# A fused relu and gate on VectorE for the first experts, their first bias folded into the output bias, and a new prologue order

## What is computed

```python
# block 1: messages with a sensitivity weight computed from adj
sens    = exp(-(1/adj - 1)**2 / (2*0.5*0.5))
weights = where(adj < 1.0, sens, 0.0)
x = x + weights @ (ln(x) @ W + B)
# block 2: 8 experts, hidden 256, top 2
logits  = z @ Wg + bg + bias                      # z = ln(x)
combine = one_hot(top2) * softmax(top2 logits)    # 1354 x 8
h = relu(einsum('td,edh->teh', z, W1) + b1)
y = einsum('teh,ehd->ted', h, W2) + b2
x = x + einsum('ted,te->td', y, combine)
# block 3: graph attention with 3 heads and two GRU cells over adj
# block 4: 8 experts, hidden 341, top 2, silu(h1) * h3
```

## Time and profile before

| what | value |
|---|---|
| median of 3 runs | 576.27 us (575.78 to 577.69) |
| the profiled execution, its own time | 573.15 us |
| its span | 571.4 us |
| PE busy | 492.5 us, 86% of the span |
| weight loads | 306.4 us, 54% |
| DVE busy | 387.3 us, 68% |
| ACT busy | 271.6 us, 48% |
| POOL busy | 118.1 us, 21% |
| mean granted TensorE clock | 0.94 of full speed |
| chain that ended last | PE 56%, DVE 24%, ACT 10%, issue 8% |

### The profile page before, as it was taken

The page is one execution under the profiler, slowest core; times in us unless marked ns, Lnnn a source line. Parts: engine busy times, 40 slices in busy tenths (PEclk is TensorE's granted clock), DMA queues, the critical chain, the costliest instruction groups (busy, mean ns, idle before and its releaser), DMA issues.

```text
span 571.4 us, 6186 instructions
## 1 busy us (share of the span) xinstructions
PE 492.5 (86%) x1889; PEld 306.4 (54%) x1889; DVE 387.3 (68%) x715; ACT 271.6 (48%) x445; POOL 118.1 (21%) x181
## 2 busy tenths in 40 slices
PE   5564879677879999999889998998978799999997
PEld 4322535344546645455444443445545687788896
DVE  2989987756586722267568868778856966666664
ACT  5988694758765421222422122111236544454553
POOL 3000000000010000000000058730103455555554
PEclk9696699889799999999999998999988999999999
DMA  8960000000000010000000013210000000000000
GB/s 284 317 170 1 1 0 0 1 1 0 1 1 1 5 45 1 0 2 0 1 0 1 28 49 103 65 30 1 0 5 2 0 2 0 20 1 2 19 1 13
DMA packets 13076, 16.76 MB, mean 29 GB/s; under 512 B 2007, under 2 KB 8410, under 8 KB 13038
## 3 DMA queue, kind: packets, MB, share of 16 engines
q1 hardware_dynamic: 13038, 16.30, 9.1%
HBM read 15.60 MB, written 0.69 MB: 29 GB/s over the span
## 4 chain that ended last, share of the span: by engine, by line
PE 56%; DVE 24%; ACT 10%; issue 8%; POOL 1%; DVEq 0%; POOLq 0%; ACTq 0%
PE bank L1220 9%; PE bank L886 7%; PE bank L888 7%; PE bank L887 7%; PE bank L1050 4%; PE bank L1168 3%; DVE pr_ring L1818 3%; PE bank L1019 2%; PE bank L1209 2%; DVE y_units L1379 2%; DVE y_units L1368 2%; PE bank L915 2%; DVE t_units L1374 2%; DVE hr_ring L1634 2%; DVE y_units L1389 1%
## 5 line engine op out<-in xcount | busy, mean ns | idle before, releaser
L1220 PE MATMUL bank<-pr_ring,hW 128*128 128x512 f32 (+3 forms) x198 | 95.5, 568 | 7.2 <-DVE pr_ring L1818 6.7
L1818 DVE SCALAR_TENSOR_TENSOR pr_ring<-adjT,regR,bank 128x512 f32<-128x512 f32 (+3 forms) x99 | 64.9, 680 | 29.5 <-PE bank L1209 27.8
L1929 DVE TENSOR_TENSOR adjT<-adjT,bank 128x512 f32<-128x512 f32 (+1 forms) x66 | 41.2, 624 | 45.5 <-PE bank L1324 24.0
L866 ACT ACTIVATE adjT<-bank 128x512 f32<-128x512 f32 (+1 forms) x66 | 36.2, 549 | 54.1 <-PE bank L888 54.1
L886 PE MATMUL bank<-z3hi,w13hi 128*128 128x512 f32 (+4 forms) x132 | 50.8, 385 | 8.2 <-DVE pr_ring L1933 3.2
L1220 PEld LDWEIGHTS bank<-pr_ring,hW 128*128 128x128 f32 (+1 forms) x198 | 35.7, 197 | 37.0 <-issue 17.8
L915 PE MATMUL bank<-y_units,msg 128*128 128x512 f32 (+3 forms) x66 | 33.3, 638 | 20.5 <-DVE y_units L1389 20.5
L888 PE MATMUL bank<-z3hi,w13lo 128*128 128x512 f32 (+4 forms) x132 | 49.4, 374 | 0.0
L887 PE MATMUL bank<-z3lo,w13hi 128*128 128x512 f32 (+4 forms) x132 | 49.0, 371 | 0.0
L1019 PE MATMUL bank<-hr_ring,W2s 128*128 128x512 f32 (+1 forms) x96 | 46.2, 569 | 0.0
L548 POOL TENSOR_TENSOR prr_ring<-adjT,adjTr 128x512 fp32r<-128x512 f32 (+4 forms) x34 | 36.0, 1060 | 48.8 <-ACT adjTr L858 46.8
(11 more groups left out here) (272 smaller groups left out, 1039.3 us busy)
## 6 DMA issues: line engine op xcount, KB each, us to landing
stage<-in_w SPq DMA_DIRECT2D x8, 341.0 KB, 3.0
adjT<-in_adjT SPq DMA_DIRECT2D x1, 2560.0 KB
...
```

The costliest lines, as they stand in the source:

```text
L866: nc.scalar.activation(s1_buf(q)[0:r, 0:w], B_H1[q % 2][0:r, 0:w], ACT.Silu).then_inc(s["s_silu"], 1)
L1220: nc.tensor.matmul(B_ACC[:, 0:w], hW[0:r, j, k * P:(k + 1) * P], ring[0:r, 0:w], start=(k == 0 and j == 0), stop=(k == K - 1 and j == T - ...
L1818: nc.vector.scalar_tensor_tensor(out=pr_ring[0:r, 4 + p % R_RING, 0:w], in0=adjT[0:r, j, cols(c)], scalar=g_col[0:r, j, k:k + 1], in1=B_F[ ...
L1929: nc.vector.tensor_tensor(sg, sg, B_GATE1[n % 2][0:r, 0:w], ALU.mult).then_inc(s["s_gated"], 1)
```

## The change

1. **Relu and gate in one DVE operation.** relu(h + b1) equals max(h, -b1) + b1, so gate times relu is gate x max(h, -b1) plus gate x b1. DVE now computes gate x max(h, -b1) straight from the hidden bank (L1673 of the changed kernel, with `nb1` = -b1 as the scalar of each partition). The relu on ACT is gone.
2. **The gate comes from on-chip memory.** ACT copies each expert's gate out of its bank once (L753, `gate_sb`, 2 buffers, 24 copies in all). PE makes the gate of expert g + 1 in the first step of expert g, and at the start of a chunk both g and g + 1 (`ahead`).
3. **The first bias goes behind the down projection.** gate x b1 times W2 is a constant row of each expert times the gate, so it is added to b2: 16 small products of W2 and b1 on PE (`hidden_bias`, L1013, between the sums of unit 2 and unit 3), a copy on ACT (L725), a transpose on PE (`hidden_bias_rows`, L1019, between the sums of unit 4 and unit 5) and an addition on DVE (L1637, between cutoff(4) and cutoff(5)), ahead of the splitting of b2.
4. **Waits.** PE overwrites a bank of `B_H` when DVE has gated tile q - 3, no longer when ACT has read it. The ring `hr_ring` has 4 buffers instead of 6.
5. **Prologue.** SP issues the first adj transfer before x, and the second before W and B. ACT waits for POOL's first 12 constants (`const_raw`) instead of all (`const_set`), does log and inverse root of unit 0 before the squares of the centred x, and square(1) of the units behind the second of those. The small copy `sel16` on DVE moves back behind newton_product(4).
6. **Tables.** PE0, ACT0, DVE0 and the MAIN tables are written anew: tasks move by a step or two.

```diff
-RING0 = 6
+RING0 = 4
+RINGG = 2
...
 PE0 = {
-    0: [("turn", 0)], 1: [("v",)], 3: [("unit", 6)], 4: [("unit", 7)], 6: [("unit", 8)], 7: [("unit", 9)], 11: [("unit", 10), ("unit", 11)],
+    0: [("turn", 0)], 3: [("unit", 6)], 5: [("unit", 7), ("v",), ("unit", 8)], 7: [("unit", 9)], 8: [("unit", 10)], 11: [("unit", 11)],
...
+        def ahead(q):
+            g, e, m = q // M0, q // M0 % E, q % M0
+            if m:
+                return []
+            return [x for x in ((g, g + 1) if e == 0 else (g + 1,)) if x // E == g // E]
...
                 for i in range(3):
                     sp.dma_start(adjT[:, 2 * i:2 * i + 2, cols(0)],
...
+                    if i == 0:
+                        sp.dma_start(xT[:, :], xT_d).then_inc(s["x_in"], 16)
+                    if i == 1:
+                        sp.dma_start(Wl0[:, :], W_d).then_inc(s["wts0_in"], 16)
+                        sp.dma_start(rowW[0:1, 0:P], B_d).then_inc(s["wts0_in"], 16)
...
-            act.wait_ge(s["const_set"], CONSTS)
+            act.wait_ge(s["const_raw"], RAW_CONSTS)
             rec_square(0)
+            rec_log(0)
+            rec_first(0)
             square_first(0)
-            rec_log(0)
             square_first(1)
-            rec_first(0)
+            rec_square(1)
             square_first(2)
-            rec_square(1)
...
             rec_first(5)
+            act.wait_ge(s["ffn0_in"], 80)
+            nc.scalar.mul(nb1[:, :], b1c[:, :], -1.0).then_inc(s["b2_step"], 1)
+            act.wait_ge(s["b2_step"], 2)
+            nc.scalar.copy(b2t[:, :], bk[1][:, 0:2 * E]).then_inc(s["b2_step"], 1)
             argument(4)
...
-                at(act, "h_ps", q + 1)
-                at(act, "y_mm", q - RING0 + 1)
-                nc.scalar.activation(hr_ring[:, q % RING0, 0:w], B_H[q % 3][:, 0:w], ACT.Relu,
-                                     bias=b1c[:, e * M0 + m:e * M0 + m + 1]).then_inc(s["h_relu"], 1)
+                for g in ahead(q):
+                    at(act, "gate_ps", g + 1)
+                    at(act, "h_gated", (g - RINGG + 1) * M0)
+                    nc.scalar.copy(gate_sb[:, g % RINGG, 0:w], B_GATE[g % 2][:, 0:w]).then_inc(s["gate_set"], 1)
...
+            def hidden_bias():
+                pe.wait_ge(s["ffn0_in"], 80)
+                pe.wait_ge(s["msg_set"], C)
+                pe.wait_ge(s["b2_step"], 1)
+                for e in range(E):
+                    for m in range(M0):
+                        mm = nc.tensor.matmul(bk[1][:, e:2 * E:E], W2s[:, e, m, :],
+                                              b1c[:, e * M0 + m:e * M0 + m + 1].to_broadcast([P, 2]), start=(m == 0), stop=(m == M0 - 1))
+                mm.then_inc(s["b2_step"], 1)
+
+            def hidden_bias_rows():
+                pe.wait_ge(s["b2_step"], 3)
+                nc.tensor.matmul(bk[4][0:2 * E, 0:P], b2t[:, :], ident[:, :], start=True, stop=True).then_inc(s["b2_step"], 1)
...
-            sums(0)
-            sums(1)
-            for g in range(2, UNITS_C):
+            for g in range(UNITS_C):
+                if g == 3:
+                    hidden_bias()
+                if g == 5:
+                    hidden_bias_rows()
                 sums(g)
...
-                at(pe, "h_relu", q - 2)
+                at(pe, "h_gated", q - 2)
...
-                if m == 0:
+                for g in ahead(q):
                     at(pe, "gt_set", c + 1)
-                    at(pe, "h_gated", (q // M0 - 1) * M0)
-                    nc.tensor.matmul(B_GATE[q // M0 % 2][:, 0:w], sel16[:, e:e + 1].to_broadcast([P, P]), GT0[:, c % 2, 0:w],
+                    at(pe, "gate_set", g - 1)
+                    nc.tensor.matmul(B_GATE[g % 2][:, 0:w], sel16[:, g % E:g % E + 1].to_broadcast([P, P]), GT0[:, c % 2, 0:w],
                                      start=True, stop=True).then_inc(s["gate_ps"], 1)
...
             newton_step(5)
+            cutoff(4)
             dve.wait_ge(s["ffn0_in"], 80)
+            dve.wait_ge(s["b2_step"], 4)
+            nc.vector.tensor_tensor(b2x[0:2 * E, :], b2x[0:2 * E, :], bk[4][0:2 * E, 0:P], ALU.add).then_inc(s["b2_step"], 1)
+            cutoff(5)
+            dve.wait_ge(s["b2_step"], 5)
             nc.vector.tensor_copy(b2hi[:, :], b2x[:, :]).then_inc(s["b2_split"], 1)
-            cutoff(4)
-            cutoff(5)
...
-                at(dve, "gate_ps", q // M0 + 1)
-                at(dve, "h_relu", q + 1)
-                hr = hr_ring[:, q % RING0, 0:w]
-                nc.vector.tensor_tensor(hr, hr, B_GATE[q // M0 % 2][:, 0:w], ALU.mult).then_inc(s["h_gated"], 1)
+                at(dve, "gate_set", q // M0 + 1)
+                at(dve, "h_ps", q + 1)
+                at(dve, "y_mm", q - RING0 + 1)
+                if q == 0:
+                    dve.wait_ge(s["b2_step"], 1)
+                nc.vector.scalar_tensor_tensor(out=hr_ring[:, q % RING0, 0:w], in0=B_H[q % 3][:, 0:w],
+                                               scalar=nb1[:, e * M0 + m:e * M0 + m + 1], in1=gate_sb[:, q // M0 % RINGG, 0:w],
+                                               op0=ALU.max, op1=ALU.mult).then_inc(s["h_gated"], 1)
```

More of the change, by code:

```diff
@@ L112 @@
[L112 to L117 removed]
+    19: [("center", 2, 0), ("sq", 17), ("arg", 14), ("ln", 17), ("exp", 14), ("inv", 17), ("neg", 1)], 20: [("arg", 15), ("exp", 15)],
@@ L118 @@
     19: [("center", 2, 0), ("mult", 15), ("step", 15), ("sign", 16)], 20: [("mult", 16), ("cut", 14), ("step", 16)],
[L119 to L121 removed]
+    21: [("sign", 17), ("scale", 2, 0), ("cut", 15), ("mult", 17)], 22: [("step", 17), ("cut", 16)], 23: [("diag", 0), ("cut", 17)],
```

82 lines of the change are left out of this document (40 added, 42 removed).

## The result

The changed kernel takes **578.75 us** (median of 18 runs, 575.78 to 582.93) against 575.62 us before (18 runs, 572.58 to 578.25). The ratio is **1.0058, 95% interval 1.0036 to 1.0080**: slower by 3.3 us by the ratio. The forecast was 570.8 us, in the wrong direction. The profiled execution took 578.04 us, with a span of 576.3 us; PE is busy 498.5 us (87%), DVE 392.6 (68%), ACT 255.6 (44%). ACT worked 16 us less than before, and the kernel is slower.

The account below looks back on a forecast made before the run. Before 198 us it saw DVE limiting block 2's first chunk, latencies the second, PE nearly the third. Terms -0.8 + 4.0 - 3.2 - 0.5 - 4.5 - 0.5 = -5.5 took 576.27 to 570.8 us; range 564.5 to 579.

Parts of the forecast that it names:

- The folded bias: Prologue: 32 records delay ACT's copy and the chain to x1(0), a loss of 4.0 us (bounds 0 and 7.2).
- Chunk 0: Block 2, first chunk, DVE the limit: most DVE waits for relus go, gain 3.2 us (bounds -0.7 and 4.9).
- Chunk 1: Block 2, second chunk: earlier gate product shortens PE's 4.51 us wait and the half clock behind it, gain 4.5 us.
- Chunk 2: Block 2, third chunk: PE is the limit, so only 0.5 us gained (0 to 2).
- Prologue start: Start of the prologue: first adj transfer issued first lets ACT begin earlier, gain 0.8 us (bounds 0 and 2.2).
- Layer norm and router: Between chunks, 97.3 to 112 us: one wait on a relu goes, gain 0.5 us (0 to 1).
- Fused operation: Gate step on DVE: 743 ns against 683, so 0.06 us more each (bounds 0 and 2.9 us in all).
- ring of 4: Buffers between gating and down projection: the needed down projection is done a step before, so no cost.
- Block 3: Last block: new task order changes nothing, covered by PE's work; zero (bounds -1.5 and +1.5 us).
- Slower: PE is tied to DVE: Block 2 rival: banks free only after DVE gates, taking back the gain; 579.5 us if all; 20%.
- The gain and the loss cancel: Rival: fold's products at half clock lose 7.2 us, second chunk of block 2 gains only 2.2; 576.3 us, 15%.
- The clock holds: Rival: fold's products keep full clock beyond 42.6 us, some 3 us less; 567.8 us, 5%.

Follow-up runs that it names:

- start_only: Kernel before with only the new prologue start (first adj transfer ahead, ACT's new order of first squares, later sel16 cast); 575.16 us, ratio 0.9989.
- act_head: Changed kernel with unit 9's square and logarithm ahead of the first gate copies and unit 11's exponential at tile 8; 575.50 us, ratio 0.9990.
- the two kernels with WARM: late_head, without and with unit factors 12 and 13 earlier on ACT, each computing hidden products of tiles 16 and 32 five times; 570.40 and 562.21 us.
- late_head: Changed kernel with act_head's two moves and the folded bias moved into PE's later waits; 571.27 us, ratio 0.9920.
- late_head_warm: late_head with the hidden products of tiles 16 and 32 computed five times instead of once; 570.40 us, ratio 0.9894.

## Why the prediction was wrong

**The folded bias** (4.0 lost): mechanism right, with every step of the chain where it was drawn; size somewhat small. It measures 5.0 us in time. The term "the sums of unit 4, 1.9 with start" took full clock for granted: in four of the five profiles with the whole fold in this place they ran at half clock for all or most of their time, and the transposition, the addition and cutoff(5) queue behind them. A is 15.1 on average over those five, and 10.2 over the eight without it there; B, 16.1 on average against 15.5, adds 0.6. The half clock itself is not the fold's alone: in five of the eight profiles without it there, the last sums before x1(0) ran at half clock too, for some 3 us, with A 10.45 to 10.63 instead of 9.51 to 9.60. With the fold standing between the units, such a stretch costs more when it falls on unit 4. The bounds (0 to 7.2) held. "Nothing downstream hides it" held too.

**Chunk 0** (3.2 gained): the step that failed. It gained nothing, C 39.14 before and 39.15 to 39.27 in the six profiles with the changed order. Against start_only it is worse: with the same relus and a clock of 1.00 from 80 to 95 us, its two last waits were one of 0.85 us, and C is 37.43. So against that profile the change *cost* some 1.7 us here, and 1.6 of the 4.9 us that I counted on the earlier trace rows hung on the clock of one execution. The sentence at fault is "The ACT copies are one expert ahead and hide behind DVE". It weighed the length of the copies (they measure 0.58 us), not their place. An operation that waits for the router stands first in ACT's queue, where one stood that waited for nothing late, and the table puts unit 11 behind another. act_head, which moves these two places only, gives 3.5 us. Of the 4.9 us of waits that went, 4.2 came back as waits for L615, and the fused operation took its 16 x 0.06 = 1 us (the forecast had 0.7, too little for 16 tiles). That closes to within half a microsecond. Of the 8.8 us between the forecast (-5.5) and the result (+3.3) this step is the largest part, 3.2 to 4.9 us.

**Chunk 1** (4.5 gained): right in kind, somewhat large. D is 40.16 and 39.53 in the two profiles with relus and 36.0 to 37.0 in the nine with the new operation and the change's order in that chunk: 3.3 us on average. The wait of 4.51 us with its half clock was there again in start_only (4.49 us) and is gone in the changed kernel.

**Chunk 2** (0.5 gained): wrong sign. At full clock E is 31.60 before and 32.27 to 32.30 with the fused operation (act_head and the two kernels with WARM), 0.7 us more. The forecast saw room on DVE and gave a small gain. The 3.4 us that after lost here against before are for the most part the clock (34.98 against 32.3). The fall needs no change: it came in a kernel with relus as well (start_only, E 33.25), and in the profile of before it happened not to. Whether the change makes it more frequent or longer is open: PE's wait ahead of it grew from 2.3 to 2.6 us, and two profiles with relus are too few to tell. I read one profile's 1.00 in this stage as a property of the kernel.

**Prologue start** (0.8 gained): 0.4 us at the sums of unit 2, and not to be told from nothing in the time. **Layer norm and router** (0.5 gained): x1(1) to gates is 14.24 before and 14.37 after; nothing. **Fused operation** (0.06 each), **ring of 4**: 744 ns as taken, and no wait on the ring in the profile. **Block 3**: from x2(2) to the end 373.2 us before and 374.3 after, within the 371.7 to 376.1 that all profiles show.

With the measured terms (start, A, B, chunk 0, chunk 1, chunk 2): -0.4 + 5.0 + 0.6 + 0 to 1.7 - 3.3 + 0.7 = 2.6 to 4.3 us; measured 2.4 and 3.3.

**The rivals.** "Slower: PE is tied to DVE" gave 579.5 us, near the result, by the wrong mechanism. PE's waits for L1673 ahead of hidden products are 2.2 us in 2 times, below the 5 us that I had set (the weight loads ahead of them waited 5.7 us in 7 times, but PE itself stood idle for those 2.2 only), and act_head and late_head gain with this tie in place. "The gain and the loss cancel" is nearer in size than the forecast, and names chunk 1 and half clock, not ACT's queue. "The clock holds" did not come: PE was busy with the 32 small products from 34.33 to 38.17 us, the clock was 0.50 from 38 to 40 us, right behind them, as in start_only without them, and 0.54 in the window from 46.30 us. There the rule of the Trainium skill (TensorE: Matmul & The Clock Gate, What's actually happening), that activity releases the clock, does not match these rows. With wide hidden products inside the router waits (late_head_warm) the clock stayed at 1.00 from 110 to 118 us. There the rule matches.
